# Normalised rows in a macaron transformer block: GpSimd's two-input tiles become one-input tiles, one chunk goes to ScalarE, and ScalarE's tiles move to other groups of attention

## The reference, cut to what matters

```python
x = x + 0.5 * ffn(layernorm(x))       # x is 16 x 256 rows of 256 values
x = x + attn(layernorm(x))
x = x + 0.5 * ffn(layernorm(x))

def layernorm(x, eps=1e-05):
    m = jnp.mean(x, -1, keepdims=True); v = jnp.var(x, -1, keepdims=True)
    return (x - m) / jnp.sqrt(v + eps)

def ffn(x):                           # wu, wg: ternary(256 -> 1024), wd: ternary(1024 -> 256)
    return (silu(x @ wu.T) * (x @ wg.T)) @ wd.T

def attn(x):                          # 16 query heads, 4 groups of keys and values, 16 wide, causal
    scores = q @ k.T / 4, masked above the diagonal
    return softmax(scores) @ v
```

## Time and profile before

| what | value |
|---|---|
| time, median of 3 runs | 611.13 us (611.11 to 612.34) |
| span of the profiled execution, first to last instruction | 610.4 us |
| PE busy | 566.9 us (93%) |
| DVE busy | 485.1 us (79%) |
| ACT busy | 411.1 us (67%) |
| POOL busy | 184.6 us (30%) |
| mean granted TensorE clock | 0.997 of full |

### The profile page before, as it was taken

One profiled execution on the slowest core, in us unless ns is written; L12 is line 12 of the kernel. 1 busy time (PEld: TensorE's weight loads), 2 busy tenths in 40 slices (PEclk: granted clock), 3 DMA queues, 4 the chain that ended last, 5 costly groups with the idle time before them and its releaser, 6 DMA issues.

```text
span 610.4 us, 12447 instructions
## 1 busy us (share of the span) xinstructions
PE 566.9 (93%) x4276; PEld 346.0 (57%) x4276; DVE 485.1 (79%) x1854; ACT 411.1 (67%) x776; POOL 184.6 (30%) x231
## 2 busy tenths in 40 slices
PE   2869999999989989999899989998899999999998
PEld 2336566555656855656565656554445655666665
DVE  6998978989866889888988987888298687856654
ACT  4637765765635368898889888887866656665741
POOL 3115101110510234555545454557731011101100
PEclk9999999999989999999999999999999999999999
DMA  8601001100205161414141424230111111211112
GB/s 317 207 18 36 18 19 35 35 19 18 36 8 119 24 134 55 91 54 91 55 90 56 91 62 88 84 58 4 36 35 34 53 53 36 69 50 56 35 35 70
DMA packets 71679, 37.90 MB, mean 62 GB/s; under 512 B 33984, under 2 KB 71104, under 8 KB 71616
## 3 DMA queue, kind: packets, MB, share of 16 engines
q1 hardware_dynamic: 71616, 37.11, 23.9%
HBM read 18.22 MB, written 10.49 MB: 47 GB/s over the span
## 4 chain that ended last, share of the span: by engine, by line
PE 79%; DVE 12%; ACT 6%; issue 2%; DMA 1%; DVEq 0%
PE bank L1107 32%; PE bank L1119 17%; PE bank L1206 7%; PE bank L1270 6%; PE bank L1261 5%; PE bank L1233 5%; PE bank L1284 2%; PE bank L1275 2%; DVE hl L847 2%; ACT shared L587 2%; DVE sm_out L969 2%; DVE hid L832 2%; DVE stats L711 1%; PE bank L1098 1%; PE bank L1244 1%
## 5 line engine op out<-in xcount | busy, mean ns | idle before, releaser
L969 DVE CUSTOM_DVE_ANT_0 sm_out<-bank,mask 128x256 f16<-128x256 f32 (+1 forms) x512 | 153.0, 352 | 28.3 <-PE bank L1233 26.4
L477 ACT ACTIVATE silu<-bank,w_scale 128x512 f32<-128x512 f32 x128 | 87.3, 682 | 117.5 <-PE bank L1107 117.5
L832 DVE SCALAR_TENSOR_TENSOR hid<-silu,h_unit,bank 128x512 f32<-128x512 f32 x128 | 95.0, 742 | 63.4 <-ACT silu L477 63.2
L587 ACT ACTIVATE shared<-bank,qk_scale 128x512 f32<-128x512 f32 x192 | 121.2, 675 | 22.7 <-PE bank L1261 22.0
L1119 PE MATMUL bank<-wT_down,hh 128*128 128x256 f16 x512 | 118.7, 273 | 5.5 <-DVE hl L847 5.3
L1119 PE MATMUL bank<-wT_down,hl 128*128 128x256 f16 x512 | 118.7, 273 | 0.0
L847 DVE TENSOR_TENSOR hl<-hid,hh 128x512 f16<-128x512 f32 x128 | 102.9, 804 | 0.0
L1107 PE MATMUL bank<-xh,wT_gate 128*128 128x512 f16 x256 | 97.1, 379 | 4.8 <-DVE hid L832 4.8
L409 POOL TENSOR_TENSOR xnl<-xn,xnh 128x1024 f16<-128x1024 f32 x14 | 30.1, 2150 | 233.9 <-ACT xn L514 199.0
L1107 PE MATMUL bank<-xh,wT_up 128*128 128x512 f16 x256 | 98.0, 383 | 1.2 <-DVE xl L776 1.2
L1107 PE MATMUL bank<-xl,wT_up 128*128 128x512 f16 x256 | 97.9, 383 | 0.0
(11 more groups left out here) (113 smaller groups left out, 751.3 us busy)
## 6 DMA issues: line engine op xcount, KB each, us to landing
q_st<-q_scratch SPq DMA_DIRECT2D x32, 256.0 KB
q_scratch<-q_hl SPq DMA_DIRECT2D x16, 256.0 KB, 2.2
out_dram<-x SPq DMA_DIRECT2D x7, 512.0 KB, 2.9
x<-in_x_dram SPq DMA_DIRECT2D x1, 3072.0 KB, 15.8
k_scratch<-k_hl SPq DMA_DIRECT2D x16, 128.0 KB, 2.4
k_st<-k_scratch SPq DMA_DIRECT2D x16, 128.0 KB
x<-in_x_dram SPq DMA_DIRECT2D x2, 512.0 KB, 4.4
shared<-in_w_up_t_dram SPq DMA_DIRECT2D x2, 512.0 KB, 6.1
```

Of the source, the lines that this page charges most:

```text
L477: act.activation(silu[:, e % 2, :], U[e % 2][:, :], ACT.Silu, scale=w_scale[:, 0:1]).then_inc(silu_ready, 1)
L587: act.activation(prob[:, place % 2, i, :], ST[(3 * place + i) % 2][:, :], ACT.Exp, scale=qk_scale[:, 4:5]).then_inc(exp_done, 1)
L832: dve.scalar_tensor_tensor(out=hid[:, e % 4, :], in0=silu[:, e % 2, :], scalar=h_unit[:, 0:1], in1=GT[e % 2][:, :], op0=ALU.mult, op1=ALU. ...
L969: ins = dve.tensor_tensor_reduce(sm_out[:, i, cols], SM[i][:, cols], mask[:, S - size:S], 1.0, MASKED, ALU.add, ALU.max, rowmax[:, seq_par ...
```

## The change

Three edits:

1. `NORM_PLACES` of ScalarE goes from (0,3), (1,0), (1,2), (1,3) to (0,1), (0,3), (1,1), (1,3).
2. GpSimd's chunks 8, 9 and 17 are written by four tensor_scalar instructions of 128x256, one per tile, which subtract the mean and multiply by `rstd` in one pass, with both as scalars per partition. In chunk 17 `xnh` is then a copy of `xn`.
3. Chunk 10 goes from GpSimd to ScalarE, as four tiles of `normed_tile` at the start of attention, behind the load of the table for exp.

```diff
-            def centre_chunk(q, t0, last_read, count):
+            def normed_chunk(q, last_read, count):
                 n, at = batch_of(q)
                 pool.wait_ge(ln_rstd, RSTD_STEPS * (n + 1))
                 pool.wait_ge(last_read, count)
-                pool.tensor_tensor(xn[:, :, :], x[:, t0:t0 + TT, :], mv[:, n, at:at + TT, 0:1].to_broadcast([P, TT, D]),
-                                   ALU.subtract).then_inc(xn_centred, 1)
-                centred[0] += 1
-
-            def scale_chunk(q):
-
-                n, at = batch_of(q)
-                pool.wait_ge(xn_centred, centred[0])
-                pool.tensor_tensor(xn[:, :, :], xn[:, :, :], rstd[:, n, at:at + TT].unsqueeze(2).to_broadcast([P, TT, D]),
-                                   ALU.mult).then_inc(xn_ready, 1)
...
+                for t in range(TT):
+                    ins = pool.tensor_scalar(xn[:, t, :], x[:, TT * (q % NC) + t, :], mv[:, n, at + t, 0:1],
+                                             rstd[:, n, at + t:at + t + 1], ALU.subtract, ALU.mult)
+                ins.then_inc(xn_ready, 1)
...
-            def normed_parts(n, q, t0, last_read, count):
-
-                centre_chunk(q, t0, last_read, count)
-                k, at = batch_of(q)
-                pool.wait_ge(xn_centred, centred[0])
+            def normed_parts(n, q, last_read, count):
+
+                normed_chunk(q, last_read, count)
+                pool.wait_ge(xn_ready, q + 1)
                 pool.wait_ge(xh_ready, 16 * n)
-                pool.tensor_tensor(xnh[:, :, :], xn[:, :, :], rstd[:, k, at:at + TT].unsqueeze(2).to_broadcast([P, TT, D]),
-                                   ALU.mult).then_inc(xnh_ready, 1)
-                pool.wait_ge(xnh_ready, n)
-                scale_chunk(q)
+                pool.tensor_copy(xnh[:, :, :], xn[:, :, :]).then_inc(xnh_ready, 1)
                 low_part(n, q)
...
-            normed_chunk(NC, 0, xnl_ready, NC - 1)
-            normed_chunk(NC + 1, TT, tr_ready, 4)
-            centre_chunk(NC + 2, 2 * TT, tr_ready, 6)
+            normed_chunk(NC, xnl_ready, NC - 1)
+            normed_chunk(NC + 1, tr_ready, 4)
             max_rest(0, 0)
-            scale_chunk(NC + 2)
             max_rest(0, 1)
...
-            NORM_PLACES = [(0, 3), (1, 0), (1, 2), (1, 3)]
+            NORM_PLACES = [(0, 1), (0, 3), (1, 1), (1, 3)]
...
                 act.activation(silu[:, 0, 0:1], silu[:, 0, 0:1], ACT.Exp)
+                for t in range(TT):
+                    normed_tile(NC + 2, 6, t)
                 key_high(1)
```

5 lines of the change are left out of this document (1 added, 4 removed).

## The result

| | kernel before | changed kernel |
|---|---|---|
| time, median of 4 runs | 611.12 us (611.08 to 612.34) | 607.06 us (606.56 to 607.55) |
| ratio | | 0.9923, 95% interval 0.9903 to 0.9942 |
| span of the profiled execution | 610.4 us | 604.9 us |
| mean granted TensorE clock in it | 0.997 | 1.000 |

The change saves 4.1 us of the median and 5.5 us of the profiled span. I forecast 8.0 of both.

What follows compares the result with a forecast made beforehand. TensorE, 79% of the chain, was taken as the bound, with time to be had only where it waits. 3.9 + 1.3 + 2.8 = 8.0 us took the span from 610.4 to 602.4, hence 603.1 us, range 600.5 to 607.4.

Steps and rivals of the forecast that it cites:

- Place A: Last chunk of phase 0, where TensorE waits 2.96 us for `hl` of VectorE, held up by GpSimd: gain 3.9 us.
- rival 4: GpSimd takes the two scalars by a slow path, even at 1.3 us per tile, 615.8 us at 2.1; chance 0.04.
- Place B: Start of phase 1, where GpSimd's work stretches VectorE and TensorE later waits 0.41 and 1.19 us: gain 1.3 us.
- Chunk 10: Its four ScalarE tiles, about 2.0 us, fit an idle time of 2.80 with 0.8 spare: cost nothing.
- Place C: Groups of attention, where TensorE waits 1.3 us a chunk for ScalarE's exponentials: moving ScalarE's tiles gains 2.8 us.
- 0.49 per chunk: Attention: taking the tile from (1,2) brings exponentials 0.49 us forward where TensorE waits 0.9, counted in every chunk.
- The median lies 0.7 above the span: Whole kernel: the forecast span of 602.4 us becomes a median time of 603.1.
- so I also count the 1.7: Last chunk of phase 0: with TensorE's wait cut to 0.8, the 1.7 us lost to the lower clock is gained too.
- 1 (tile as dear as a two-input one): GpSimd's tile costs 0.74 us, as a two-input instruction does: 607.4 us; chance 0.17.
- 2 (clock falls all the same): Last chunk of phase 0: a wait of 0.8 us or more still lowers TensorE's clock: 604.8 us; chance 0.15.
- 3 (a new wait at (1,1)): Attention: the tile at (1,1) delays three exponentials, then row maxima; gain there 0.5 us, not 2.8: 605.4; chance 0.12.
- 5: No change: gains at the last chunk of phase 0 and start of phase 1 are waited away in attention, 611; chance 0.02.

Runs made afterwards that it cites:

- run 1: Kernel before with only chunks 8 and 9 normalised by GpSimd's one-input tiles: 608.32 us, ratio 0.9953.
- run 5: Kernel before with GpSimd's chunks 8 and 9 still two-input tensor_tensor, but cut into pieces of 128x256: 610.39 us, ratio 0.9976.
- run 6: Changed kernel with chunks 8, 9 and 17 each given another tensor_scalar form, rows not properly normalised, only durations and places read: span 603.8 us.
- run 8: Changed kernel with chunk 17's rows and their high and low parts made by VectorE, not GpSimd: 605.74 us, ratio to before 0.9899.
- Run 3: Kernel before with only chunk 10 moved from GpSimd to four tiles of ScalarE: 612.51 us, ratio 1.0011.
- run 2: Kernel before with only the places of ScalarE's four tiles in attention changed: 610.76 us, ratio 0.9983.
- Runs 7 and 9: Changed kernel with VectorE's Newton steps moved from (1,0), (1,1) to (1,2), (1,3): 607.31 us; or packed into (0,3) and (1,0): 605.97 us.

## Why the prediction was right or wrong

The forecast was faster, 603.1 us within 600.5 to 607.4. It came out faster, at 607.1: sign right, size half, near the range's upper end. By its steps:

**Place A: gain right in the profiled pair, its cause half wrong.** Forecast 3.9, measured 4.44 (run 1 alone gives the same), 1.7 of it from a clock that most executions behind the median did not lose. That VectorE is held up by GpSimd, that TensorE's wait goes with it and the clock then stays at 1.00 were right. That the gain still came out near the forecast is luck, as two errors cancelled. The step "I take 0.45, near the one-input line" mis-sized the tile: 1.21 us. And "at worst they wait for all four tiles" took the tile for an instruction that holds VectorE up like the others; it hardly does (0.17 us at a time), and its form counts, not its length (run 5). By the forecast's own rule for rival 4, 4 us lost for each us above 0.85, a tile of 1.21 would have made A 1.4 us slower; the rule rests on the hold-up and fell with it. The Trainium skill (SBUF — State Buffer, section "Who interferes with whom") says that a VectorE instruction with two SBUF inputs contends with a GpSimd instruction that reads SBUF. Here a GpSimd tensor_tensor does (0.54 us for a 0.17 us step, run 5) and holds it to its own end; a tensor_scalar that reads SBUF as well adds at most 0.17 us to such a step in the changed kernel and lets an `hl` of 0.75 run wholly beside it. So the rule fits the one form and not the other; the measurement decides. A further 0.37 us was lost at chunk 8's transposes, late by the slow tiles (run 6).

**Place B: wrong.** Forecast 1.3, measured a loss of 0.19. The step that failed is "xnl begins 2.9 us behind": the tiles took 4.82 and not 1.8, the copy 1.42 and not 1.1, so `xnl` begins 6.4 us behind the first of them (432.80 to 439.19), and it and `add_output`, the instructions that hold VectorE up, came no earlier. The step "covers the waits of 1.6 but for the last" was sound: with chunk 17 off GpSimd, 1.35 us came (run 8), with 0.44 of the last wait left where I had left 0.3. The place was right and the tool was not.

**Chunk 10: right.** 2.06 us in an idle time of 2.80, with 0.83 left, forecast 2.0 and 0.8; the stretch with it takes 23.49 us in every kernel. Run 3 has 0.2 us more that I cannot place.

**Place C: half.** Forecast 2.8, measured 1.38 (run 2: 1.03 in five chunks alone). For the odd chunks 0.45 each was counted, and 0.40, 0.38 and 0.36 came. The step that failed is "0.49 per chunk" for the even ones: 0.08 came. ScalarE's part held, with one wait of 0.9 cut to 0.39. But from 291.25 to 298.2 us VectorE has no idle time above 0.04, and what was late next was its row maxima, 0.61 us, 0.41 of it by the mask that now meets the `shift` step. The prediction had seen VectorE's `q_hl` bound the other tile's gain there, and did not apply the same reasoning to this one. Runs 7 and 9 show that the wait hangs on where VectorE's steps stand: with the steps late it goes and returns as 0.78 at the end, with the steps ahead of VectorE's idle time it falls to 0.24.

**From the span to the time: wrong.** "The median lies 0.7 above the span" compared one execution with the median of others. The executions of the kernel before that were run beside the experiments fall in groups by their mean granted clock: 20 of 45 at 1.000 with spans of 608.9 to 609.5, 23 at 0.997 with 610.3 to 610.7, 2 at 0.994 with 612.3 and 612.4. The profiled one was of the second. In the profiled one the clock was below 1.00 behind the gap of place A and nowhere else. So its 1.7 us cannot be had in every execution, and between the groups the span differs by some 1.2; three of the four executions behind the first median, at 611.08 to 611.13, fit the group without it. In the kernels with chunk 9 by tensor_scalar all executions are at 0.999 or 1.000. Also, two of the changed kernel's four have spans of 605.7 and 605.8, not 604.9; the profile shows only one of them, and what differs stays open. With 609.4 for the before of the median and 605.3 for the mean after, the gain is 4.1, as measured. By places it is 2.8 for A (run 1), 1.4 for the attention and 0.2 lost at B: 4.0. For the time, then, the term that failed at A is "so I also count the 1.7".

Added up, the span came out at 604.9 and not 602.4: A 0.5 better, B 1.5 worse, C 1.4 worse. One sum in the forecast does not come out: 0.8 more at A and half of what is left to C's bound, 1.4, put the lower end of the range at 600.9 and not 600.5.

**The rivals.** 1 (tile as dear as a two-input one): the price is even higher than its 0.74, but its mechanism, VectorE waiting for the tiles, did not appear; that 607.4 is near the result is chance. 2 (clock falls all the same): no. 3 (a new wait at (1,1)): there is one, but in the even chunks and for VectorE, not for ScalarE's exponentials in the odd ones. 4 (slow tile): its condition came true at A, its effect did not; the reason stands under place A. 5: no.

## What to carry to other kernels

When one engine's instruction stretches another's, ask first which forms do it: replacing a GpSimd tensor_tensor by a slower tensor_scalar took 2.8 us off the gap, and 1.7 more where the clock had fallen behind it, while cutting it into shorter tensor_tensors took off 0.7. The number of inputs does not tell the forms apart: the masks have one, and hold VectorE up. When a wait is removed inside a loop, look along the other engines for the next place without idle time, and at what the earlier work will now meet: work moved ahead of an idle time of VectorE gained 0.28 us a chunk, moved behind it gained nothing. And before a gain that rests on a fallen clock is put into a forecast, look at whether every execution has it.

## What was not expected of the hardware

- A GpSimd tensor_scalar on 128x256 takes 1.21 us with two operations and two scalars per partition, 0.84 with one operation and a constant; the tensor_tensor of run 5 on the same shape takes 0.61 when nothing holds it. One input is not cheaper than two here. The Trainium skill (GPSIMD Engine Reference, section 3.1) has about 1.8 cycles per element at 1.2 GHz for the best case of a tight loop, an estimate of 0.38 us; no tensor_scalar measured here comes within twice that.
- The tensor_scalar leaves VectorE's two-input instructions nearly alone, while tensor_tensor and the masks hold them to their own end. Why was not tried. The tiles yield instead where an `hl` runs beside their start: 1.72 us, against a minimum of 1.21. For the CAST (437.69, 1.42 us) no run tells: the one `hl` beside it was begun 0.16 us ahead of it, and the CAST itself took 1.04 in run 6.
- The kernel before, the same program each time, had a mean clock of 1.000 in 20 of 45 executions and less in the others. In run 5, whose profiled execution shows 0.63 behind a wait of 2.17 us, it was 1.000 in seven of ten. The waits of the executions that were not profiled are not known.
